# The small network's first layer and router in halves of fp32r

## What is computed

```python
x = x + gru(segment_sum(h[src] + relvec[type], dst), h)   # h = layernorm(x), layer 0's graph part
x = x + small_network(layernorm(x))                       # layer 0's feed-forward part
x = x + (segment_sum((h @ W.T + b)[src], dst)) / (deg + 1)  # layer 1's graph part, W is L1_gnn_W
x = x + experts(layernorm(x))                             # layer 1's feed-forward part, 2 of 8 experts
```

```python
a  = relu(h1 @ sW1 + sb1)              # shared: 256 -> 256, then 128, then 256
ae = relu(h1 @ eW1[e] + eb1[e])        # four experts: 256 -> 128, then 64, then 256
gates = softmax(h1 @ gW + gb)          # router: 256 -> 4; the two largest are taken, softmax of them
```

## Time and profile before

| | |
|---|---|
| profiled execution, its own time | 3448.99 us |
| its span | 3447.4 us, mean granted clock 0.767 |
| three runs | 3440.41 / 3451.92 / 3462.8 us |
| TensorE busy (matmul / weight load) | 2345.9 us (68%) / 1576.6 us (46%) |
| VectorE, ScalarE, GpSimd busy | 45%, 24%, 56% |

### The profile page before, as it was taken

One profiled execution on the slowest core, in us unless ns is written; L12 is line 12 of the kernel. 1 busy time (PEld: TensorE's weight loads), 2 busy tenths in 40 slices (PEclk: granted clock), 3 DMA queues, 4 the chain that ended last, 5 costly groups with the idle time before them and its releaser, 6 DMA issues. The chain is left out here.

```text
span 3447.4 us, 47206 instructions
## 1 busy us (share of the span) xinstructions
PE 2345.9 (68%) x11708; PEld 1576.6 (46%) x11709; DVE 1535.9 (45%) x4138; ACT 830.1 (24%) x1644; POOL 1915.7 (56%) x2043
## 2 busy tenths in 40 slices
PE   1478888888876666353666665454443379999996
PEld 1245555555542443131333332221211179999996
DVE  7444444555444334113455544322312056666663
ACT  2233333333231121021111000000000035555543
POOL 0364445455665666635666666666666545655553
PEclk6588989889897777566677666665565589999998
DMA  5232222222232233213333333333333443333334
GB/s 165 87 86 62 63 61 74 68 78 82 84 89 86 84 90 88 80 51 102 97 100 93 93 100 92 89 95 90 91 96 93 119 121 71 73 72 73 72 48 105
DMA packets 163077, 298.23 MB, mean 87 GB/s; under 512 B 47543, under 2 KB 106656, under 8 KB 162752
## 3 DMA queue, kind: packets, MB, share of 16 engines
q0 software_dynamic: 96736, 235.19, 26.2%
q1 hardware_dynamic: 41476, 39.54, 3.7%
q10 hardware_dynamic: 24732, 22.06, 2.1%
HBM read 255.78 MB, written 47.27 MB: 88 GB/s over the span
## 5 line engine op out<-in xcount | busy, mean ns | idle before, releaser
L755 POOL DMA_INDIRECT rows<-table,srcT x1568 | 1544.6, 985 | 1026.2 <-issue 505.1
L821 PE MATMUL bank<-rows,onehot 128*128 x1952 | 670.5, 484 | 685.0 <-POOLq L743 409.0
L821 PEld LDWEIGHTS bank<-rows,onehot 128*128 x1952 | 217.4, 111 | 1101.1 <-issue 975.3
L781 DVE SCALAR_TENSOR_TENSOR onehot<-iota_row,tbase,dstT 128x512 f16 x488 | 366.5, 753 | 685.5 <-issue 439.8
L1895 ACT ACTIVATE hid<-bank,b 128x256 f32<-128x256 f32 x432 | 179.1, 465 | 290.8 <-PE bank L1847 270.4
L1845 PE MATMUL bank<-W_high,hid_high 128*128 128x256 f32 x864 | 244.8, 283 | 0.0
L1845 PE MATMUL bank<-xe_high,W_high 128*128 128x256 f32 x864 | 241.2, 279 | 4.9 <-DVE xe_low L1928 4.9
L1847 PE MATMUL bank<-xe_high,W_low 128*128 128x256 f32 x864 | 240.1, 278 | 0.0
L1846 PE MATMUL bank<-xe_low,W_high 128*128 128x256 f32 x864 | 240.1, 278 | 0.0
L1846 PE MATMUL bank<-W_low,hid_high 128*128 128x256 f32 x864 | 239.8, 278 | 0.0
L1847 PE MATMUL bank<-W_high,hid_low 128*128 128x256 f32 x864 | 239.8, 278 | 0.0
(11 more groups left out here) (348 smaller groups left out, 3803.5 us busy)
## 6 DMA issues: line engine op xcount, KB each, us to landing
rows<-table,srcT POOLq DMA_INDIRECT x1568
W<-in_L_ffn_W_dram SPq DMA_DIRECT2D x14, 1024.0 KB
x_res<-in_x_dram SPq DMA_DIRECT2D x1, 6144.0 KB, 22.6
normal<-xn ACTq DMA_DIRECT2D x11, 528.0 KB
table<-part ACTq DMA_DIRECT2D x11, 512.0 KB
totals<-x_res SPq DMA_DIRECT2D x11, 512.0 KB, 6.8
table<-part SPq DMA_DIRECT2D x6, 512.0 KB, 2.9
table<-part_b SPq DMA_DIRECT2D x6, 512.0 KB, 2.9
```

The source lines that it names most:

```text
L755: nc.gpsimd.indirect_dma_start(out=rows[:, k % (M * U), 0:ROW], out_offset=None, in_=q.table, in_offset=bass.IndirectOffsetOnAxis(srcT[:, ...
L781: last = nc.vector.scalar_tensor_tensor(onehot[:, ds(slot, U), :], iota_row[:, :].unsqueeze(1).to_broadcast([P, U, P]), base, dstT[:, ds(k ...
L821: last = nc.tensor.matmul(acc[:, 0:ROW], hots[:, ds(hot0 + s * P, P)], ring_rows[:, ds(row0 + s * ROW, ROW)], start=False, stop=False, ski ...
```

## The change

The raw `sW1`, `eW1` and `gW` are loaded into the ring's space and split into halves in the setup, by three copies on ScalarE and three subtractions on VectorE. In `d3` ScalarE writes `h1_high` (it uses the space of `red_high`), and VectorE makes `h1_low` by `dve_low` as the first thing of `dve_d3`. TensorE's order in `d3` becomes: block 0 of the first layer as six fp32r products, of which the last two wait for `h1T_low`; the router as six products a tile of four columns; then blocks 1 to 5 as six products each. Layer 1's `W` is loaded at the start of layer 1, turned in `pe_e0` of its group 0 and scaled at the head of `dve_e1` of its group 0; the filling of `place` by GpSimd moves from the setup to layer 1's start. Buffers `place`, `to_list`, `from_list` and `gcnT` move to the scopes where they are used.

```diff
-        sW1 = wt("sW1", [P, C, D])
-        eW1 = wt("eW1", [P, E0, C, P])
-        gW = wt("gW", [P, C, E0])
+        sW1 = split_wt("sW1", [P, C, D])
+        eW1 = split_wt("eW1", [P, E0, C, P])
+        gW = split_wt("gW", [P, C, E0])
...
+        sW1_raw = ring_words[:, 12 * D:14 * D].rearrange("p (c o) -> p c o", o=D)
+        eW1_raw = ring_words[:, 14 * D:18 * D].rearrange("p (e c o) -> p e c o", c=C, o=P)
+        gW_raw = ring_words[:, 18 * D:18 * D + C * E0].rearrange("p (c o) -> p c o", o=E0)
...
-                nc.gpsimd.iota(place[:, :], pattern=[[P, NT], [0, 2]], base=1, channel_multiplier=1)
...
-                load(wraw[2][:, :, :], a["L1_gnn_W"].rearrange("(j p) i -> p j i", p=P))
...
+                nc.scalar.activation(gW[0][:, :, :], gW_raw, ACT.Copy).then_inc(raw_high, 1)
+                nc.scalar.activation(sW1[0][:, :, :], sW1_raw, ACT.Copy).then_inc(raw_high, 1)
+                nc.scalar.activation(eW1[0][:, :, :, :], eW1_raw, ACT.Copy).then_inc(raw_high, 1)
...
+                dve.wait_ge(raw_high, RAW_HIGH)
+                nc.vector.tensor_tensor(gW[1][:, :, :], gW_raw, gW[0][:, :, :].bitcast(F32), ALU.subtract)
+                nc.vector.tensor_tensor(sW1[1][:, :, :], sW1_raw, sW1[0][:, :, :].bitcast(F32), ALU.subtract)
+                nc.vector.tensor_tensor(eW1[1][:, :, :, :], eW1_raw, eW1[0][:, :, :, :].bitcast(F32), ALU.subtract)
...
-                for c in range(C):
-                    turned += 1
-                    dve.wait_ge(raw_turned, turned)
-                    nc.vector.tensor_scalar(gcnT[:, c, :], bank[(turned - 1) % 6][:, 0:D], 1.0 / SCALE, None,
-                                            ALU.mult).then_inc(raw_copied, 1)
...
-                for n, blocks in enumerate((6, 6, 2)):
+                for n, blocks in enumerate((6, 6)):
...
+        h1_high, h1_low = red_high, red_low
...
         def pe_d3(pe, g, w):
             n = w * P
             turn(g, w, 0, 3, "h1_ready", "h1T_ps", pe)
-            pe.wait_ge(S["h1T_sb"], g + 1)
-            for i in range(w):
-                o = slice(i * E0, (i + 1) * E0)
-                for c in range(C):
-                    last = nc.tensor.matmul(bank[2][:, o], t0[:, c, i * P:(i + 1) * P], gW[:, c, :],
-                                            start=i == 0 and c == 0, stop=c == C - 1, skip_group_check=True)
-            last.then_inc(S["gate_ps"], 1)
+            pe.wait_ge(S["h1T_high"], g + 1)
             for j, b in enumerate(L1_BANKS):
                 if j >= 4:
                     pe.wait_ge(S["l1_act"], 6 * g + j - 3)
-                for c in range(C):
-                    w1 = sW1[:, c, j * P:(j + 1) * P] if j < 2 else eW1[:, j - 2, c, :]
-                    last = nc.tensor.matmul(bank[b][:, 0:n], w1, t0[:, c, 0:n], start=c == 0, stop=c == C - 1)
+                steps = [(half, moving, c) for half, moving in ((0, h1_high), (1, h1_high), (0, h1_low)) for c in range(C)]
+                for at, (half, moving, c) in enumerate(steps):
+                    if j == 0 and at == 2 * C:
+                        pe.wait_ge(S["h1T_low"], g + 1)
+                    w1 = sW1[half][:, c, j * P:(j + 1) * P] if j < 2 else eW1[half][:, j - 2, c, :]
+                    last = nc.tensor.matmul(bank[b][:, 0:n], w1, moving[:, c, 0:n], start=at == 0, stop=at == len(steps) - 1)
                 last.then_inc(S["l1_ps"], 1)
+                if j == 0:
+                    for i in range(w):
+                        o = slice(i * E0, (i + 1) * E0)
+                        for at, (half, still, c) in enumerate(steps):
+                            last = nc.tensor.matmul(bank[2][:, o], still[:, c, i * P:(i + 1) * P], gW[half][:, c, :],
+                                                    start=i == 0 and at == 0, stop=at == len(steps) - 1, skip_group_check=True)
+                    last.then_inc(S["gate_ps"], 1)
...
-                last = nc.scalar.activation(t0[:, c, 0:w * P], bank[b][:, 0:w * P], ACT.Copy)
+                last = nc.scalar.activation(h1_high[:, c, 0:w * P], bank[b][:, 0:w * P], ACT.Copy)
...
         def dve_d3(dve, chain, g, w):
+            dve_low(dve, g, w, h1_low, h1_high, 0, 3, "h1T_high", "h1T_low")
             dve.wait_ge(S["gate_ps"], g + 1)
...
         def pe_e0(pe, g, w):
+            if isinstance(g, int) and g == 0:
+                pe.wait_ge(R["gcn_loaded"], 16)
+                for c in range(C):
+                    for j in range(C):
+                        last = nc.tensor.transpose(bank[2][:, c * D + j * P:c * D + (j + 1) * P],
+                                                   gcn_raw[:, j, c * P:(c + 1) * P], ident[:, :])
+                last.then_inc(R["gcnT_ps"], 1)
             pe.wait_ge(q2.evacuated, first_window(g) + w)
...
             pe.wait_ge(R["sumsT_sb"], g + 1)
+            if isinstance(g, int) and g == 0:
+                pe.wait_ge(R["gcnT_ready"], 1)
...
             if isinstance(g, int) and g == 0:
+                dve.wait_ge(R["gcnT_ps"], 1)
+                nc.vector.tensor_scalar(gcnT[:, :, :], bank[2][:, :].rearrange("p (c o) -> p c o", o=D), 1.0 / SCALE, None,
+                                        ALU.mult).then_inc(R["gcnT_ready"], 1)
                 dve_split_first(dve, 0, 0)
...
+                nc.gpsimd.iota(place[:, :], pattern=[[P, NT], [0, 2]], base=1, channel_multiplier=1)
                 nc.gpsimd.iota(from_list[:, :], pattern=[[1, LCOLS]], base=0,
...
+                act.dma_start(gcn_raw[:, :, :], a["L1_gnn_W"].rearrange("(j p) i -> p j i", p=P)).then_inc(R["gcn_loaded"], 16)
                 load_raw(act, 0)
```

More of the change, by code:

```diff
@@ L104, in program @@
         inv_deg = sb("inv_deg", [P, NT], F32)
-        place = sb("place", [P, NT * 2], I32)
-        to_list = sb("to_list", [P, LCOLS], I32)
-        from_list = sb("from_list", [P, LCOLS], I32)
         lists = sb("lists", [1, 3 * E1 + 1], I32)
@@ L221, in program @@
         Wr = sb("Wr", [P, C, E1], F32, graph)
-        gcnT = sb("gcnT", [P, C, D], F32, graph)
         br = sb("br", [P, E1], F32, graph)
@@ L288, in program @@
         ring_words = rows[:, :, :].rearrange("p s d -> p (s d)").bitcast(F32)
-        wraw = [ring_words[:, j0 * D:j1 * D].rearrange("p (j i) -> p j i", i=D) for j0, j1 in ((0, 6), (6, 12), (12, 14))]
+        wraw = [ring_words[:, j0 * D:j1 * D].rearrange("p (j i) -> p j i", i=D) for j0, j1 in ((0, 6), (6, 12))]
+        sW1_raw = ring_words[:, 12 * D:14 * D].rearrange("p (c o) -> p c o", o=D)
+        eW1_raw = ring_words[:, 14 * D:18 * D].rearrange("p (e c o) -> p e c o", c=C, o=P)
+        gW_raw = ring_words[:, 18 * D:18 * D + C * E0].rearrange("p (c o) -> p c o", o=E0)
         sW3_raw, eW3_raw, b_l3_raw, b_l3_low = (sb(name, [P, k, D], F32, setup)[:, :, :] for name, k in
@@ L335, in program @@
         EDGE_LOADS = 9
+        RAW_HIGH = 6
         with nc.Block() as block:
@@ L421, in _ @@
                 load(bhh[:, :], a["L0_gnn_b_hh"].rearrange("(j p) -> p j", p=P))
-                load(sW1[:, :, :], a["L0_ffn_sW1"].rearrange("(c p) o -> p c o", p=P))
+                load(sW1_raw, a["L0_ffn_sW1"].rearrange("(c p) o -> p c o", p=P))
                 load(sW2[:, :, :], a["L0_ffn_sW2"].rearrange("(c p) o -> p c o", p=P))
@@ L425, in _ @@
                 for e in range(E0):
-                    load(eW1[:, e, :, :], a["L0_ffn_eW1"][e].rearrange("(c p) o -> p c o", p=P))
+                    load(eW1_raw[:, e, :, :], a["L0_ffn_eW1"][e].rearrange("(c p) o -> p c o", p=P))
                 load(eW2[:, :, :], a["L0_ffn_eW2"].rearrange("e p o -> p e o"))
                 load(eW3_raw[:, :, :], a["L0_ffn_eW3"].rearrange("(q r) k o -> (r k) q o", r=2))
-                load(gW[:, :, :], a["L0_ffn_gW"].rearrange("(c p) o -> p c o", p=P))
+                load(gW_raw, a["L0_ffn_gW"].rearrange("(c p) o -> p c o", p=P))
                 load(Wr[:, :, :], a["L1_ffn_Wr"].rearrange("(c p) o -> p c o", p=P))
@@ L650, in _ @@
                             turned += 1
-                            dve.wait_ge(raw_high, 3 + turned)
+                            dve.wait_ge(raw_high, RAW_HIGH + turned)
                             o = slice(j0 * P, (j0 + k) * P)
@@ L880, in program @@
         rT, zT, tT, nT, hT = (work[:, j:j + C, :] for j in range(0, 10, C))
-        a1T, a2T, t0 = work[:, 0:6, :], work[:, 6:9, :], hT
+        a1T, a2T = work[:, 0:6, :], work[:, 6:9, :]
         red4 = sb("red4", [P, GW, D], F32, layer0)
@@ L891, in program @@
         names = ("h4_ready hT_ps high_out types_out deg_ps deg_sb redT_ps hT_high hT_low hT_sb red_high red_low r_ps z_ps in_ps hn_ps r_act z_act t1_done t2_done "
-                 "n_act hnew back_ps x1_var x1_std h1_ready h1T_ps h1T_sb gate_ps l1_ps l1_act l2_ps l2_act "
+                 "n_act hnew back_ps x1_var x1_std h1_ready h1T_ps h1T_high h1T_low gate_ps l1_ps l1_act l2_ps l2_act "
                  "lg_ready ex_ready mm_ready em_ready gates_ready gT_ps gT_sb spread_ps gated l3_ps x2_var x2_std "
@@ L1099, in act_d3 @@
             n = w * P
```

(7 more changed lines are left out.)

2 lines of the change are left out of this document (1 added, 1 removed).

## The result

The changed kernel takes 3473.94 us (median of 18 runs, 3467.3 to 3494.98), beside 3451.57 us of the kernel before (18 runs, 3440.41 to 3469.47). The ratio is 1.0065 with a 95% interval from 1.0051 to 1.0078: 22 us slower, and within one per cent. The forecast was 3491, from a sum of +41.5 us; the range held the result, but the sum was nearly twice what was measured. Both the wait and the low clock that it rests on are there; one of its terms, group 9, does not show in the time. The profiled execution took 3473.2 us (span 3471.6, mean clock 0.763, before 0.767).

What follows compares the result with a forecast made beforehand. TensorE's program was taken to bound layer 0 in groups 1 to 9, waits for rows after that. Groups +38.7, setup +1.4, group 0 +1, layer 1 +0.4 made +41.5 on 3449.0: 3491 us, range 3440 to 3512.

Steps and rivals of the forecast that it cites:

- step 2: TensorE's new wait in block 0: low half ready 4.4 us after the high one, 8.1 in group 9.
- step 1: Split products: 24 router records cost 2.7 us at full clock, 5.1 at low, 0.9 or 1.7 more than now.
- step 3: Clock low until 4.9 us into block 1; blocks 1 to 5 take 9.2 us, bounds 7.0 and 9.8.
- The softmax and choice behind the logits: VectorE's work on the logits starts 4 to 6 us later; nothing counted for it.
- Group 9: Layer 0, last group counted in full: its stage takes 23.3 us against 12.2, +11.1.
- step 4: Setup +1.4 us, exposed, from three more halves; group 0 +1; last group 0.
- step 5: Layer 1's start: place ahead of the gathers on GpSimd's queue, +0.4 us; W's load and transposes covered.
- Rival C: Not slower: the clock stays high through block 0, wait and router in groups 1 to 8; 3446 us, chance 12%.
- Rival B: Clock comes back part-way, half of router and dense stretch high, 21 us less: 3470; chance 17%.
- the 6% set against the 0.213 us: A rival given 6%; against it stood 0.213 us a router record at low clock; its claim is not in the text.
- Rival E: Worse: groups 10 and 11 not covered, +5 us each, or later gates delay nine groups by 1; 3510, chance 6%.

Runs made afterwards that it cites:

- experiment 1: Changed kernel with VectorE's subtractions for h1_low moved ahead of the next window's one-hots and the emptying, groups 0 to 10; 3441.48 us, 0.9988 of the kernel before.
- experiment 2: Changed kernel with router logits from the high halves alone, 8 products a group instead of 24; 3446.63 us, 1.0001 of the kernel before.
- experiment 9: Changed kernel with the router's operands exchanged, h1_low still made where the change puts it; 3400.12 us, 0.9990 of the kernel before on another chip.
- experiment 5: Changed kernel with groups 9 to 13 computed from the high halves alone; 3429.1 us, 1.0086 of the kernel before on another chip.
- experiment 4: Changed kernel with group 0 alone computed from the high halves; 3471.53 us, 1.0066 of the kernel before.
- experiment 3: Kernel before with only the move of layer 1's W (also called W move alone); 3447.08 us, 0.9996 of the kernel before.
- experiment 6: Changed kernel with eight f16 products filling TensorE's wait for h1_low in groups of four tiles; 3412.99 us, 1.0035 of the kernel before on another chip.
- experiment 7: Kernel with the low half first, its router moved from behind block 0 to behind block 3; 3400.77 us, 1.0001 of the kernel before on another chip.
- experiment 8: Kernel with the low half first, the router's operands exchanged, 6 wide products for 24; 3381.02 us, 0.9947 of the kernel before on another chip.

## Why the prediction was right, and where it was not

**The wait (step 2): right.** Foreseen was a low half 4.4 us after the high one and a router 5.3 us into the stage (4.4 and two products). The router began 3.9 to 6.5 us into it, on the mean 5.2; waits of 0.8 to 3.4 us, sum 17.0. The cause is VectorE's queue, as experiment 1 shows by changing nothing but the order.

**The router (step 1): right.** 5.1 us foreseen, 5.11 measured in groups 1 to 9, and 2.73 at full clock in group 10 (2.7 foreseen). From start to start a record took 0.213 us at the low clock and 0.113 at the full one; experiment 2 took out 16 products with their loads and 3.41 us went. In group 1's router, at 0.50, the weight loads were busy 4.97 of 5.00 us. No run parts a product from its load: at the low clock products of 512 columns start 0.43 us apart with 4 columns standing (experiment 9) and with 128 alike.

**The dense stretch (step 3): near.** 9.2 us for blocks 1 to 5 foreseen, 8.8 measured on the mean (8.1 to 9.6). Together a stage was foreseen at 19.5 us and took 19.1: +24.4 us in eight groups, where +27.6 stood in the sum. The softmax and choice behind the logits came 4.4 us later in group 6 (4 to 6 foreseen), and counting nothing for it was right: TensorE's waits for the gates were 4.1 us from group 1's start to group 9's, after 4.7.

**Group 9 (step 2 and 3, +11.1 us): the step that failed.** Its stage grew by 8.4 us in the first pair of traces, not 11.1, as the wait was 4.0 us and not 6 to 7. But the step that failed is its price: the text said that from group 10 on a delay is covered by the waits for rows, and charged group 9 in full. A stage's delay falls on what comes after it, and between group 9's stage and group 10's TensorE waits for rows (23.0 us before, 12.5 after). Group 9 started 28.2 us later than before and group 10 only 23.4; experiment 5 cut group 9's stage by 9 us or more, and group 10 came no earlier for it.

**Setup and group 0 (step 4, +2.4 us): there, and covered.** Group 0's stage starts at 180.2 and 179.9 us in the two traces with the setup as before, and at 181.3 to 181.9 in the changed kernel and experiments 1, 2 and 4, which is what the +1.4 foresaw. It does not reach group 1, which starts at 251.5 and 251.2 us in the first two and at 250.8 to 252.4 in experiments 1, 2 and 4 (for the changed kernel's own 263.6 see experiment 4). **Layer 1 (step 5, +0.4): right in its smallness**, experiment 3.

With these the sum is 24.4 us for the eight groups, against 22 measured. Some of it TensorE's other work gives back (from group 1's start to group 9's its recurrent products took 186.3 us after 191.1, the relation products 19.1 after 22.7), and some the waits for rows between groups 9 and 10. In the first pair the stretch from group 1's start to group 9's grew by 16.1 us only, in the pair of experiments 3 and 4 by 26.0 (stages: 28.6). Traces of the same code there lie 4.3 us (before and W move alone) and 5.6 us (the changed kernel and experiment 4) apart on that stretch, which I had not allowed for. That the sum of what was left comes so near to 22 is in part luck.

**Rival C** (the clock stays up through block 0, wait and router, 3446) did not happen. Its point was whether block 0 holds the clock across the idle time. In the changed kernel's groups 1 to 9 the clock was low (0.50) at the stage's start and never rose before the wait ended, so they do not test it. Group 1 of experiment 2 does. There the clock is full when the stage begins at 252.4 us; four products, then the wait, in which it falls (columns as in the earlier trace rows):

```profile
252.30:253.30 1.00, 0.92 (x4) 0.67 (x4) 0.92 (x3) 0.03 (x1) 0.69 (x2) 1.00 0.34 86
253.30:254.30 1.00, 0.27 (x2) 0.00 (x0) 0.86 (x3) 0.00 (x0) 0.69 (x2) 1.00 0.27 98
254.30:258.40 4.10, 0.82 (x2) 0.72 (x3) 3.11 (x7) 0.00 (x0) 3.19 (x4) 0.50 0.34 96
```

With TensorE at work through the wait, the router took 2.7 to 3.1 us in all of groups 1 to 8 (experiment 6, clock 0.85 to 1.00). Work alone did not always bring that: in groups 4, 5 and 7 of experiment 1 TensorE had not stood still and the router took 5.1 us (0.50). Rival B (3470) lies nearer to 3474 than the forecast, for the wrong reason: no router half at full clock was seen in groups 1 to 8, where the clock over it was 0.50 each time. For the 6% set against the 0.213 us, no run shows a router record below 0.213 us at the low clock. Rival E's covered groups 10 and 11 are settled by experiment 5.

## What to carry to other kernels

When a product is split into rounded halves, ask first who makes the low half and what stands ahead of it in that engine's queue; one move in VectorE's queue was worth 27 us (7 either way), at least about what the whole change cost. Price a stall of TensorE with the clock that goes with it, here 13.4 us in the router and the blocks behind it beside 17.0 us of waiting (experiment 1). And let the narrow operand stand and the wide one move, if the answer can be turned back cheaply: 6 products and 4 small transposes replaced 24 loads, and the kernel ended 0.5% faster than where it began.

## What the runs showed of the hardware

- TensorE was busy without a gap through 24 router records at the full clock and the dense products behind them, and the granted clock still fell to 0.50 near the router's end, from 0.9 us before it to 1.1 us after it, for 3.4 to 3.5 us (once 6.8). Over all traces, groups 1 to 11, this happened behind 27 of 32 such routers. It did not in group 10 of experiment 1, groups 3, 6 and 11 of experiment 6 and group 6 of experiment 7, and what set these five apart is not shown. It did not happen after 8 such records either (1.0 to 1.4 us, experiment 2, groups 9 to 11), nor after the six wide products (experiment 8). I had taken idle time for the only thing that brings it down.
- Between the traces of kernels that hardly differ up to there, group 1's start lay 12 us apart (263.6 and 251 us), and group 13's within 2 us again.
